# Scores of two halves of the heads issued as one block on four row groups of TensorE, in an attention and mixture-of-experts kernel

## What is computed

```python
def reference(x, ctx, gate_w, gate_b, w1, w3, w2):   # x, ctx: (4, 256, 128)
    # 16 heads of 8, causal with a linear bias of the distance (ALiBi)
    scores = einsum('bhtd,bhsd->bhts', heads(layernorm(x)), heads(ctx)) / sqrt(8)
    attn = softmax(scores + bias, axis=-1)           # bias is -inf for s > t
    x = x + einsum('bhts,bhsd->bhtd', attn, heads(ctx))
    h = layernorm(x)                                 # (1024, 128)
    probs = softmax(h @ gate_w + gate_b)             # 8 experts, the best 2 are used
    out_e = (silu(h @ w1[e]) * (h @ w3[e])) @ w2[e]  # 128 -> 512 -> 128
    return x + sum over the two best e of weight_e * out_e
```

## Time and profile before

| | us |
|---|---|
| runs, median (lowest to highest of 3) | 211.79 (208.49 to 213.57) |
| the profiled execution | 209.91 |
| its span | 208.1 |

### The profile page before, as it was taken

One profiled execution on the slowest core, in us unless ns is written; L12 is line 12 of the kernel. 1 busy time (PEld: TensorE's weight loads), 2 busy tenths in 40 slices (PEclk: granted clock), 3 DMA queues, 4 the chain that ended last, 5 costly groups with the idle time before them and its releaser, 6 DMA issues.

```text
span 208.1 us, 4699 instructions
## 1 busy us (share of the span) xinstructions
PE 182.2 (88%) x1559; PEld 154.2 (74%) x1559; DVE 124.4 (60%) x406; ACT 84.5 (41%) x155; POOL 81.3 (39%) x152
## 2 busy tenths in 40 slices
PE   7898999999999899999795888997999999999600
PEld 7765777867777577776574677996899999999500
DVE  2899967797769977699458345850333333333205
ACT  2425758376552665526711617320333332323100
POOL 5498893270203606523605110663033333322400
PEclk9999999999999999999859699999999999999955
DMA  5400014699990780100201526328788998800055
GB/s 180 127 3 25 27 14 25 157 203 237 204 178 19 216 236 17 42 0 13 67 1 32 221 53 210 146 74 254 250 290 284 274 307 278 264 28 28 25 149 167
DMA packets 33975, 27.70 MB, mean 133 GB/s; under 512 B 8624, under 2 KB 29744, under 8 KB 33952
## 3 DMA queue, kind: packets, MB, share of 16 engines
q1 hardware_dynamic: 32560, 24.36, 45.3%
q0 software_dynamic: 1248, 2.57, 3.5%
q10 hardware_dynamic: 144, 0.48, 0.6%
HBM read 19.18 MB, written 7.82 MB: 130 GB/s over the span
## 4 chain that ended last, share of the span: by engine, by line
PE 57%; DVE 20%; DMA 8%; issue 7%; POOL 5%; ACT 1%; SPq 1%; POOLq 0%; DVEq 0%; ACTq 0%
PE banks L745 17%; PE banks L759 7%; PE banks L531 6%; PE banks L484 5%; PE banks L537 4%; DVE neg_max L1223 3%; PE banks L509 3%; PE banks L540 3%; PE banks L496 3%; DMA w_up<-in_up 2%; POOL slots L1072 2%; PE banks L477 2%; PE banks L556 2%; DMA tokens<-in_x 2%; DMA v_pad<-results 2%
## 5 line engine op out<-in xcount | busy, mean ns | idle before, releaser
L745 PE MATMUL banks<-xst,w_up 128*128 128x128 f32 x368 | 45.2, 276 | 2.7 <-DMA w_up<-in_up 1.5
L745 PEld LDWEIGHTS banks<-xst,w_up 128*128 128x128 f32 x368 | 42.9, 192 | 3.5 <-issue 1.8
L1131 POOL DMA_INDIRECT results<-y,xs x23 | 22.1, 960 | 40.2 <-DVE y L1501 39.6
L1495 DVE TENSOR_TENSOR hid<-silu,banks 128x512 f32<-128x512 f32 x23 | 15.8, 687 | 31.0 <-PE banks L745 31.0
L941 ACT ACTIVATE silu<-banks 128x512 f32<-128x512 f32 x23 | 13.7, 597 | 32.3 <-PE banks L745 32.3
L484 PE MATMUL banks<-cb 128*128 128x256 bf16 x128 | 25.0, 277 | 0.8 <-ACT qk_t L828 0.3
L759 PE MATMUL banks<-w_down,hid 128*128 x184 | 24.7, 277 | 1.1 <-DVE y L1501 0.7
L1072 POOL DMA_INDIRECT slots<-xm,place_i x16 | 16.9, 1056 | 21.4 <-DVE xm L1349 8.0
L844 ACT ACTIVATE probs<-banks 128x768 f32<-128x768 f32 x20 | 16.2, 811 | 20.0 <-PE banks L513 15.6
L759 PEld LDWEIGHTS banks<-w_down,hid 128*128 128x128 f32 x184 | 22.3, 192 | 1.9 <-issue 1.9
L531 PE MATMUL banks<-probs_whole,v_whole 128*72 128x256 f32 (+1 forms) x96 | 20.7, 365 | 1.7 <-ACT o_t L877 0.9
(11 more groups left out here) (139 smaller groups left out, 308.9 us busy)
## 6 DMA issues: line engine op xcount, KB each, us to landing
w_up<-in_up SPq DMA_DIRECT2D x23, 512.0 KB, 4.7
slots<-pads SPq DMA_DIRECT2D x8, 520.0 KB, 10.0
w_down<-in_L_ffn_w SPq DMA_DIRECT2D x8, 256.0 KB, 4.6
xs<-slots SPq DMA_DIRECT2D x23, 65.0 KB, 3.7
v_pad<-results SPq DMA_DIRECT2D x4, 256.0 KB, 3.7
k_in<-in_ctx SPq DMA_DIRECT2D x4, 128.0 KB, 3.4
v_in<-in_ctx SPq DMA_DIRECT2D x4, 128.0 KB, 3.3
out<-tokens SPq DMA_DIRECT2D x4, 128.0 KB, 1.8
```

Source lines behind the costliest of these rows:

```text
L745: last = nc.tensor.matmul(ps[:, j * P:(j + 1) * P], w_up[t % UP_BUFFERS][:, m * FFN + j * P:m * FFN + (j + 1) * P], xst[t % 2][:], start=T ...
L1131: nc.gpsimd.indirect_dma_start(out=results, out_offset=bass.IndirectOffsetOnAxis(xs[:, t, TARGET_COL:TARGET_COL + 1].bitcast(I32), 0), in_ ...
L1495: nc.vector.tensor_tensor(hid[t % 2][:], silu[t % 2][:], u_ps[t % 2], ALU.mult)\
```

## The change

The two functions for scores are cut into a wide and a narrow part each, and a third puts them together: `scores_for_both(exp_g, half, max_g)` computes scores for exponentials of one half and scores for maxima of the other half, on all four row groups, into four banks. Its order is four masks, two wide ones for exponentials, two wide ones for maxima, two narrow ones and two narrow ones. In step n the first joint block has exponentials of half 0 of step n + 1 with maxima of half 1 of step n + 2, the second has exponentials of half 1 of step n + 1 with maxima of half 0 of step n + 3. Each waits for all that either part waited for. The scores for maxima of half 1 of the third group are no longer computed before the first step.

VectorE's order follows: in step n it takes the maxima of half 1 of step n + 2 (count n + 3) and splits them first, then forms the low part, places the turned maxima and takes the maxima of half 0 of step n + 3. In the last batch the low part of step 14 is formed ahead of giving places, no longer in step 14 itself.

```diff
+            def scores_for_both(exp_g, half, max_g):
+
+                masked(s2[half], cb[:, 2, :])
+                masked(s1, cb[:, 1, :])
+                wide_for_exp(exp_g, half)
+                wide_for_maxima(max_g, 1 - half, s1)
+                narrow_for_exp(exp_g, half)
+                narrow_for_maxima(max_g, 1 - half, s1)
...
-            pe.wait_ge(max_done[1], 2)
-            scores_for_maxima(2, 1, first_s1[2][1])
             pe.wait_ge(max_split, 2)
             turn_max()
...
                         pe.wait_ge(q_max_ready, n + 2)
                         pe.wait_ge(exp_done[0], after(n + 1))
-                        scores_for_exp((g + 1) % GROUPS, 0)
+                        if more[2]:
+                            pe.wait_ge(max_done[0], n + 3)
+                            pe.wait_ge(max_done[1], n + 2)
+                            scores_for_both((g + 1) % GROUPS, 0, (g + 2) % GROUPS)
+                        else:
+                            scores_for_exp((g + 1) % GROUPS, 0)
...
-                    if more[3] and g % 2 == 0:
-                        pe.wait_ge(max_done[1], n + 3)
-                        pe.wait_ge(stack_kept, n + 4)
-                        scores_for_maxima((g + 3) % GROUPS, 0)
...
                     values(n, 0)
-                    if more[3] and g % 2:
-                        pe.wait_ge(max_done[1], n + 3)
-                        pe.wait_ge(stack_kept, n + 4)
-                        scores_for_maxima((g + 3) % GROUPS, 0)
...
                     if more[1] and more[3]:
                         pe.wait_ge(exp_done[1], after(n + 1))
-                        scores_for_exp((g + 1) % GROUPS, 1)
+                        pe.wait_ge(max_done[1], n + 3)
+                        pe.wait_ge(stack_kept, n + 4)
+                        scores_for_both((g + 1) % GROUPS, 1, (g + 3) % GROUPS)
                     pe.wait_ge(low_done[1], n + 1)
                     values(n, 1)
-                    if more[3]:
-                        pe.wait_ge(max_done[0], n + 4)
-                        scores_for_maxima((g + 3) % GROUPS, 1)
...
-            for n in range(3):
+            for n in range(2):
                 maxima(0, n + 1, first_s1[n][0])
...
-                    low_probs(g, n)
+                    if more[2]:
+                        maxima(1, n + 3)
+                        split_maxima(n + 3)
+                    if not (last_one and g == 2):
+                        low_probs(g, n)
...
-                    if more[3]:
-                        maxima(0, n + 4)
                     if more[2]:
                         place_maxima((g + 2) % GROUPS, n + 3)
...
                     if more[3]:
-                        maxima(1, n + 4)
-                        split_maxima(n + 4)
+                        maxima(0, n + 4)
...
                     if last_one and g == 1:
+                        low_probs(g + 1, n + 1)
                         give_places(LAST - 1)
```

23 lines of the change are left out of this document (17 added, 6 removed).

## The result

The changed kernel took 214.72 us (median of 4 runs, 212.14 to 220.03), the kernel before beside it 210.84 (208.49 to 213.57). The ratio is 1.018, with a 95% interval of 1.012 to 1.024: about 3.9 us slower by the medians, which lies inside the 2% that the prediction called "within", with the interval's end outside.

A forecast was written before the change was run, and what follows sets the result against it. TensorE bounds the first three attention batches, VectorE close behind. Won 3.1 and 1.6, given back 5.45: 0.8 us longer, 210.7 in the profiled measure, 212.5 as median; range 206.5 to 217.5.

The forecast's parts named there:

- Joint block 0.93, four groups together: TensorE's joint block of scores: four row groups overlap as two do, 0.93 us for two blocks of 0.69 before.
- 12.2 us of TensorE's time saved: 27 joint blocks each save 0.45 us of TensorE's time; at best all of it is won.
- An even step is therefore 5.00: Even attention steps: the walked chain of joint blocks, VectorE reductions, split and turn takes 5.00 us.
- odd 6.06: Odd attention steps: TensorE's longer queue after the second block makes 6.06 us; with even steps, batch 0 takes 22.1.
- Batch 1 24.3, batch 2 24.9; 3.1 won in three batches: Batches 0 to 2 if undisturbed: batch 1 24.3 against 25.62, batch 2 24.9 against 26.07; 3.1 us won in all.
- GpSimd's keys at the batch starts, 0.8 twice: Batch starts: GpSimd building keys lengthens VectorE's small SBUF operations on the chain, 0.8 us twice, 1.6 given back.
- One extra fall of the clock in batches 1 or 2, 2.0: Starts of batches 1 and 2: waits for the split bring one fall to half clock, 2.0 us.
- Last scores +0.4, weights +0.55, load's slack 1.6, half a fall behind the first tile +0.9: Tail: last scores 0.4 later, weights 0.55 later, first expert tile's load has 1.6 slack, half-chance clock fall adds 0.9.
- not worth more than this slack: Last batch: moved low part ends attention some 2.5 us earlier, worth no more than the load's 1.6 us slack.
- Waits shorter than walked: Rival, attention batches: half of the 12.2 us comes through, 205.7 us; chance 0.19.
- Four groups don't run together: Rival, joint block: four row groups run in turn, block 1.10, 4.5 us more, 217.0; chance 0.06.
- The clock falls again and again: Rival, batch 1 and 2 starts and first expert tile: three extra falls, 217.9 us; chance 0.22; sign over 12 us half clock.

The follow-up runs named there:

- experiment 2: Against experiment 1's kernel, the two blocks of a joint one issued one after the other, same order of steps: 229.19 us, 1.097 times the kernel before.
- experiment 1: Changed kernel with 14 instead of 2 clock-keeping matmuls in the prologue's opened wait (the filled kernel): 215.21 us, ratio to the kernel before 1.023.
- experiment 5: Against experiment 1's kernel, VectorE's subtraction for the next batch's queries moved behind the maxima of half 0 in the first step of batches 0 to 2: 211.66 us.
- experiment 3: Kernel before, with one prologue block of scores for maxima issued behind the turn of the second split, opening the same wait: 212.69 us.
- experiments 7 and 9: 7: experiment 1's kernel with VectorE's residual and subtraction later, low part's move undone: 210.77 us; 9: same with x normalised earlier, low part moved again: 209.28 us.

## Why the prediction came out, and which steps failed

The time (212.5 forecast, 214.72 measured, within the range) came out for partly wrong reasons, and with some luck. In the profiled executions 0.75 us longer was forecast and 3.0 measured. Up to the last batch's start 0.5 was forecast and 4.06 measured, 3.56 too little; behind it 0.25 longer was forecast and 1.06 shorter measured, an error of 1.31 the other way. A range 11 us wide took in what was left. The sum's terms in turn.

- **Joint block 0.93, four groups together.** Right: 0.91. 12.2 us of TensorE's time saved, if all of it were on the path: batch 1 of experiment 2 gives some 10; the 14.0 between the medians has falls of the clock and a collision in it. The Trainium skill's page TensorEngine Tiling (Array Packing), "Performance Considerations", was cited for the gain stopping at the reading of PSUM. Half of it is borne out: each step now hangs on VectorE's reductions out of PSUM, but most of the joining's price is real, and what took it back was the new order.
- **"An even step is therefore 5.00", "odd 6.06", batch 0 22.1.** Failed, and this is the largest error of the sum: 2.4 us. At full clock the steps of batch 0 took 6.82, 6.16, 5.34 and 6.16 (experiment 1). Two things were missing. The walk of the first step left out VectorE's subtraction for the next batch's queries, which stood ahead of the maxima on the chain and was stretched to 1.72 us by GpSimd (experiment 5 takes it off the chain and gains 0.96). In the changed kernel itself it is the low part there that GpSimd stretched, 2.58 us against the 0.95 of the other steps, which the walk did not have either. And the sentence that counted the stack for the next batch as hidden was wrong for the even step: behind its second joint block TensorE has values and stack back to back (0.91 + 0.78 + 0.72 from 34.76 to 37.17 in experiment 1's kernel), 2.41 in all, 0.29 longer than the walked way over the reduction (1.05 + 1.02 + 0.05).
- **Batch 1 24.3, batch 2 24.9; 3.1 won in three batches.** Of the 3.1, 1.6 were to be given back for GpSimd's keys, which makes 25.1 and 25.7 for these batches and 1.5 won in all. Measured 25.43 and 26.31 at full clock; with the 24.48 of experiment 1 that is 1.86 lost instead of 1.5 won. Of this error of 3.4 us, 2.4 is batch 0, 0.3 batch 1 and 0.6 batch 2: here the walk was nearly right.
- **GpSimd's keys at the batch starts, 0.8 twice.** The mechanism was right, the size a little high: small operations took 0.58 instead of 0.17 in batch 1, 0.42 and 0.57 instead of 0.16 in batch 2, 1.1 us in all against 1.6.
- **One extra fall of the clock in batches 1 or 2, 2.0.** The size was near, the place was not. In the profiled execution it came ahead of batch 0 and cost 2.6 us until batch 1. The step I did not take was to ask what the block removed from the prologue had covered: it halved a wait, 1.20 against 0.57. The term for taking that block out was nothing; at full clock it is 0.43 won, and the wait that it opens is what brings the fall (experiment 3 shows this alone). In experiment 1's profiled execution falls come at the places I named, where this one does not.
- **Last scores +0.4, weights +0.55, load's slack 1.6, half a fall behind the first tile +0.9.** +0.68, +0.16 (2.60 against 2.44 from the last scores to the first scatter) and a first tile that waits on its load: 0.55 - 1.6 = -1.05 us was forecast from the last scores to the first tile, -0.88 measured. The last term failed: TensorE waited 1.12 us there, not nearly 2, no fall came behind it, and the rest of the kernel is 0.86 shorter, since a wait for weights of 1.45 us is 0.41. This miss of 1.76 us hides half of the one on the batches.
- **The low part moved is "not worth more than this slack".** Failed as a general statement: experiments 7 and 9 give it +1.2 and -2.5 us by the medians, with half clock behind a wait of TensorE in either (115.14 in 7, 121.56 in 9), so that the clock has a part in both; how large is not shown.
- **Rivals.** "Waits shorter than walked" is out: no batch of the changed kernel was under 25 us. "Four groups don't run together" is out. "The clock falls again and again" was nearer than its chance of 0.22 says: the changed kernel's profile has 23.9 us at 1.2 GHz before 130 us, the filled one's 26.2, that of the kernel before 10.2. The prediction's own sign for this rival, half clock for more than 12 us of the attention, was met: 10.9 us in batch 0 and 6.8 in the last batch, where the kernel before had 10.2 in all.

Open: how large the clock's share of each median is. One profiled execution per kernel shows where falls came, and the spread of the runs that they don't come each time. The mean granted clock of every run bears on it: the kernel before takes 206.8 us at 0.959, about 211.1 at 0.937 and 214.3 at 0.920, and the four runs of the changed kernel are 212.14 at 0.937, 212.91 at 0.920, 216.54 at 0.922 and 220.03 at 0.877. So at a like clock it is once 1.0 us longer, once some 1.4 shorter and once nearly 3 longer (no run before is near 0.877), and a large part of its 3.9 us goes with a lower clock.
